# A two-layer decoder on one core: routing from the unnormalised sum, ranks built in another order, the last two experts normalised one by one

## The reference

```python
x = _layernorm(x + _L1_xattn_ref(x, ctx_1024, ...))        # CROSS1
probs = softmax(xf @ Wr)                                    # xf: 1024 x 128, Wr: 128 x 8
eidx = argmax(probs); p_tok = probs[eidx]
onehot = one_hot(eidx, 8)
rank = (cumsum(onehot, axis=0) - onehot)[eidx]              # tokens before this one in its expert
keep = rank < cap                                           # cap = 128
xe = xf[dispatch]                                           # 8 experts x 128 slots
ye = relu(xe @ W1) @ W2 * (p_tok[dispatch] * valid)
x = _layernorm(x + scatter_add(ye))
```

## Time and profile before

| What | Value |
|---|---|
| Median of the runs | 432.25 us (431.9 to 434.29) |
| Profiled execution, its time | 433.34 us |
| Profiled execution, span in the trace | 431.5 us |
| Mean granted clock of TensorE | 0.946 of full |
| Busy: PE, PEld, DVE, ACT, POOL | 372.1, 326.3, 282.8, 226.2, 53.8 us |

### The profile page before, as it was taken

The page is one execution under the profiler, slowest core; times in us unless marked ns, Lnnn a source line. Parts: engine busy times, 40 slices in busy tenths (PEclk is TensorE's granted clock), DMA queues, the critical chain, the costliest instruction groups (busy, mean ns, idle before and its releaser), DMA issues.

```text
span 431.5 us, 8936 instructions
## 1 busy us (share of the span) xinstructions
PE 372.1 (86%) x3188; PEld 326.3 (76%) x3188; DVE 282.8 (66%) x833; ACT 226.2 (52%) x526; POOL 53.8 (12%) x61
## 2 busy tenths in 40 slices
PE   4689898998999998999888999899999889863492
PEld 3577777886779997898876999788997677742391
DVE  6598889888955557532784455844866887825353
ACT  2145666764756565675347546584557455721241
POOL 6700005900000000000000000000002002010125
PEclk9989999999999999999969999999999979985597
DMA  5655320213330000200020000200021114700301
GB/s 162 187 182 161 111 58 17 75 54 111 122 111 2 2 2 1 74 2 2 4 71 2 2 0 2 74 2 2 1 56 32 51 24 152 230 35 0 109 13 33
DMA packets 22602, 25.14 MB, mean 58 GB/s; under 512 B 3224, under 2 KB 17313, under 8 KB 22560
## 3 DMA queue, kind: packets, MB, share of 16 engines
q1 hardware_dynamic: 21088, 22.95, 18.0%
q0 software_dynamic: 512, 0.97, 0.7%
q10 hardware_dynamic: 960, 0.66, 0.5%
HBM read 17.82 MB, written 6.83 MB: 57 GB/s over the span
## 4 chain that ended last, share of the span: by engine, by line
PE 71%; DVE 14%; issue 7%; DMA 3%; ACT 2%; POOL 1%; POOLq 0%; SPq 0%; ACTq 0%; DVEq 0%
PE bank_D L825 13%; PE bank_C L715 10%; PE bank_D L689 9%; PE bank_A L700 8%; DVE negmax L1208 4%; PE bank_A L841 4%; PE bank_A L843 3%; PE bank_A L842 3%; PE bank_D L615 2%; PE bank_D L673 2%; PE bank_A L755 2%; PE bank_D L745 1%; PE bank_A L635 1%; PE bank_A L1521 1%; PE bank_D L728 1%
## 5 line engine op out<-in xcount | busy, mean ns | idle before, releaser
L1208 DVE TENSOR_REDUCE negmax<-bank_D 128x2 f32<-128x512 f32 x192 | 127.6, 685 | 42.2 <-PE bank_D L689 42.0
L968 ACT ACTIVATE expo<-bank_A 128x512 f32<-128x512 f32 x192 | 110.3, 597 | 50.1 <-PE bank_A L700 48.0
L689 PE MATMUL bank_D<-k_head,q_sp 128*128 128x256 f32 x384 | 91.5, 324 | 10.0 <-DVE negmax L1208 5.3
L700 PE MATMUL bank_A<-q_sp,k_head 128*128 128x256 f32 x384 | 83.1, 302 | 4.9 <-DVE q_sp L1203 3.4
L1004 ACT ACTIVATE hidden<-bank_A,b 128x256 f32<-128x256 f32 x128 | 53.7, 471 | 52.1 <-PE bank_A L843 52.0
L689 PEld LDWEIGHTS bank_D<-k_head,q_sp 128*128 128x128 f32 x384 | 61.8, 200 | 22.3 <-issue 10.1
L825 PE MATMUL bank_D<-mix_w,hidden 128*128 128x128 f32 x512 | 67.8, 275 | 0.0
L700 PEld LDWEIGHTS bank_A<-q_sp,k_head 128*128 128x128 f32 x384 | 61.3, 196 | 7.7 <-DVE q_sp L1203 5.1
L825 PEld LDWEIGHTS bank_D<-mix_w,hidden 128*128 128x128 f32 x512 | 62.5, 191 | 1.6 <-issue 1.6
L715 PE MATMUL bank_C<-expo,v_aug 128*32 128x256 f32 x768 | 47.6, 389 | 2.0 <-ACT expo L968 1.6
L1267 DVE SCALAR_TENSOR_TENSOR y_mixture<-bank_D,g_w,y_mixture 128x128 f32<-128x128 f32 x64 | 22.3, 349 | 30.5 <-PE bank_D L825 28.8
(11 more groups left out here) (173 smaller groups left out, 511.1 us busy)
## 6 DMA issues: line engine op xcount, KB each, us to landing
mix_w<-in_mix_w SPq DMA_DIRECT2D x24, 256.0 KB, 3.6
k_head<-k_scratch SPq DMA_DIRECT2D x92, 48.0 KB
k_scratch<-qk_hi SPq DMA_DIRECT2D x24, 128.0 KB, 2.4
w_last<-in_mix_w SPq DMA_DIRECT2D x8, 256.0 KB, 6.4
k_scratch<-qk_lo SPq DMA_DIRECT2D x12, 128.0 KB, 2.3
proj_w<-in_proj SPq DMA_DIRECT2D x1, 640.0 KB, 5.2
xe_scratch<-empty_row SPq DMA_DIRECT2D x1, 520.0 KB, 4.7
expo<-xe_scratch SPq DMA_DIRECT2D x2, 260.0 KB, 3.2
```

Source lines behind the costliest of these rows:

```text
L689: last = mm(where(seq, b, ("max", k))[:, qt * SEQ:(qt + 1) * SEQ], q_sps[SET[seq, b]][:, k // 4, qt * P:(qt + 1) * P], k_heads[SET[seq, b] ...
L700: last = mm(where(seq, b, ("exp", h))[:, kt * SEQ:(kt + 1) * SEQ], k_heads[SET[seq, b]][:, t, g, kt * P:(kt + 1) * P], q_sps[SET[seq, b]][ ...
L968: activate(expo[:, exp_slot(seq, b, h), :], where(seq, b, ("exp", h))[:], ACT.Exp, scale=float(HD) ** -0.5).then_inc(free(seq, b, ("exp", ...
L1208: V.tensor_reduce(negmaxes[SET[seq, b]][:, s // 4, :, 32 * (s % 4)], where(seq, b, ("max", s))[:].rearrange("p (q n) -> p q n", q=QT), AX. ...
```

## The change

There are three parts. First, CROSS1 no longer transposes the normalised rows for the router but the sum before it (`transpose_sum`, step 32 instead of 34), with a router matrix whose column means are taken off. The logits are then those of the normalised rows except for the factor 1/std of the row, which doesn't alter the order; the exponential gets it later by a multiplication. Root and normalisation of CROSS1 move from steps 31 and 32 to 33 and 35, and ROUTE starts at step 34 instead of 35. Second, the counts matmuls come ahead of the wait for the onehot flags, one matmul with the triangle covers both tiles, another adds the first tile's flags to the second; the counts start at the expert's number instead of zero on each of 128 rows, so that the slot comes out of the sum directly, and are updated after the slot. The ranks move from step 2 to 3 of ROUTE, the exponential from 1 to 2; both stay at the same tick. Third, the groups of the last normalisation are 2, 2, 2, 1 and 1 experts.

```diff
 VALUES_AT = 17
-BACK_AT, CTX_AT, OUT_AT, ROOT_AT, NORM_AT, TURN_AT = 26, 28, 30, 31, 32, 34
-ATTENTION_STEPS = range(KEYS_AT, TURN_AT + 1)
+BACK_AT, CTX_AT, OUT_AT = 26, 28, 30
+ROOT_AT, NORM_AT, TURN_AT = 31, 32, 34
+SUM_TURN_AT, LAST_ROOT_AT, ROUTE_AT, LAST_NORM_AT = 32, 33, 34, 35
+ATTENTION_STEPS = range(KEYS_AT, LAST_NORM_AT + 1)
 GATE_AT, GATE_EXP_AT, GATE_WEIGHTS_AT, GATE_TURN_AT, BIAS_AT = 0, 1, 2, 4, 6
+CENTRE_AT = 3
...
     starts += [(at + len(MIXTURE_STEPS), CAUSAL1, seq) for seq, b, at in MIXTURE]
-    starts += [(at + TURN_AT + 1, ROUTE, seq) for seq, b, at in ATTENTION if b == CROSS1]
+    starts += [(at + ROUTE_AT, ROUTE, seq) for seq, b, at in ATTENTION if b == CROSS1]
...
                 turn(seq, b, "out", "D")
-            if s == TURN_AT:
+            if s == TURN_AT and b < CROSS1:
                 turn(seq, b, "xT", "A")
+            if s == SUM_TURN_AT and b == CROSS1:
+                turn(seq, b, "yT", "A")
...
                 turn(seq, b, "gate", "D")
+            if s == CENTRE_AT and (seq, b) == MIXTURE[0][:2]:
+                turn(seq, b, "centre", "D")
...
                 turn(seq, b, "logits", "D")
-            if s == 2:
+            if s == 3:
...
     c[:, C_ORDER:C_ORDER + QT * EXPERTS] = np.tile(EXPERTS - np.arange(EXPERTS), QT)
-    c[:, C_BASE:C_BASE + QT * EXPERTS] = np.tile(CAP * np.arange(EXPERTS), QT)
+    c[:, C_LIMIT:C_LIMIT + QT * EXPERTS] = np.tile(CAP * (1 + np.arange(EXPERTS)), QT)
+    c[:, C_FIRST:C_FIRST + EXPERTS] = np.arange(EXPERTS)
...
+                def transpose_sum(seq, b):
+
+                    wait_drained(pe, seq, b, "out")
+                    wait_free(pe, seq, b, "yT")
+                    for qt in range(QT):
+                        last = nc.tensor.transpose(where(seq, b, "yT")[:, qt * P:(qt + 1) * P],
+                                                   y[b][:, qt, :], ident)
+                    last.then_inc(full(seq, b, "yT"), 1)
...
                             output(seq, b, aT, wo[b])
-                        if s == TURN_AT:
+                        if s == TURN_AT and b < CROSS1:
                             transpose_x(seq, b)
+                        if s == SUM_TURN_AT and b == CROSS1:
+                            transpose_sum(seq, b)
...
                             last.then_inc(full(seq, b, "gate"), 1)
+                        if s == CENTRE_AT and (seq, b) == MIXTURE[0][:2]:
+                            pe.wait_ge(ld_const, 16)
+                            wait_free(pe, seq, b, "centre")
+                            mm(where(seq, b, "centre")[:, 0:EXPERTS], const[:, C_ONES:C_ONES + P],
+                               gate_w[:, 1, :], start=True, stop=True
+                               ).then_inc(full(seq, b, "centre"), 1)
...
                         if s == 0:
-                            wait_drained(pe, seq, CROSS1, "xT")
+                            wait_drained(pe, seq, CROSS1, "yT")
+                            wait_drained(pe, *MIXTURE[0][:2], "centre")
                             wait_free(pe, seq, b, "logits")
...
                                 last = mm(where(seq, b, "logits")[:, qt * EXPERTS:(qt + 1) * EXPERTS],
-                                          xT[seq][:, qt * P:(qt + 1) * P], gate_w[:, 1, :],
+                                          aT[:, qt * P:(qt + 1) * P], gate_c[:],
                                           start=True, stop=True)
                             last.then_inc(full(seq, b, "logits"), 1)
-                        if s == 2:
+                        if s == 3:
+                            wait_free(pe, seq, b, "rank")
+                            dst = where(seq, b, "rank")[:, 0:QT * EXPERTS]
+                            tri, ones = const[:, C_TRI:C_TRI + P], const[:, C_ONES:C_ONES + P]
+                            chosen = onehot[:, QT * seq:QT * (seq + 1), :].rearrange("p a e -> p (a e)")
+                            pe.wait_ge(counts_ready, seq + 1)
+                            for qt in range(QT):
+                                mm(dst[:, qt * EXPERTS:(qt + 1) * EXPERTS], ones, before[:, seq, :],
+                                   start=(qt == 0), stop=False)
                             pe.wait_ge(onehot_ready, seq + 1)
-                            wait_free(pe, seq, b, "rank")
-                            for qt in range(QT):
-                                dst = where(seq, b, "rank")[:, qt * EXPERTS:(qt + 1) * EXPERTS]
-                                mm(dst, const[:, C_TRI:C_TRI + P], onehot[:, QT * seq + qt, :],
-                                   start=True, stop=False)
-                                last = mm(dst, const[:, C_ONES:C_ONES + P], before[:, QT * seq + qt, :],
-                                          start=False, stop=True)
-                            last.then_inc(full(seq, b, "rank"), 1)
+                            mm(dst, tri, chosen, start=False, stop=False)
+                            mm(dst[:, EXPERTS:QT * EXPERTS], ones, onehot[:, QT * seq, :],
+                               start=False, stop=True).then_inc(full(seq, b, "rank"), 1)
...
                             copy_out(seq, b, "ctx", aT[:])
-                        if s == ROOT_AT:
+                        if s == (LAST_ROOT_AT if b == CROSS1 else ROOT_AT):
                             root(seq, b)
-                        if s == TURN_AT:
+                        if s == TURN_AT and b < CROSS1:
                             copy_out(seq, b, "xT", xT[seq])
+                        if s == SUM_TURN_AT and b == CROSS1:
+                            copy_out(seq, b, "yT", aT[:])
...
                     for s in ROUTE_STEPS:
-                        if s == 1:
+                        if s == 2:
...
                             moments(seq, b)
-                        if s == NORM_AT:
+                        if s == (LAST_NORM_AT if b == CROSS1 else NORM_AT):
...
                             weigh(seq)
+                        if s == CENTRE_AT and (seq, b) == MIXTURE[0][:2]:
+                            wait_filled(dve, seq, b, "centre")
+                            V.scalar_tensor_tensor(gate_c[:], where(seq, b, "centre")[:, 0:EXPERTS],
+                                                   -1.0 / P, gate_w[:, 1, :], ALU.mult, ALU.add
+                                                   ).then_inc(free(seq, b, "centre"), 1)
+                            V.tensor_copy(before[:, 0, :], const[:, C_FIRST:C_FIRST + EXPERTS]
+                                          ).then_inc(counts_ready, 1)
...
                     logits, diff, score, exps, work = (route[seq][:, i] for i in range(5))
-                    (greatest, first, total, weight, rank, base, beyond, number) = (
-                        route_col[seq][:, i, :] for i in range(8))
+                    (greatest, first, total, limit, number, beyond) = (
+                        route_col[seq][:, i, :] for i in range(6))
...
                     link(V.tensor_reduce(greatest, logits, AX.X, ALU.max))
-                    V.tensor_tensor(diff, logits, wide(greatest), ALU.subtract).then_inc(shifted, 1)
                     link(V.tensor_tensor(work, logits, wide(greatest), ALU.is_ge))
...
                     link(V.tensor_reduce(first, score, AX.X, ALU.max))
-                    link(V.tensor_tensor(onehot[:, tiles, :], score, wide(first), ALU.is_equal))
-                    for i in range(QT * seq, QT * (seq + 1)):
-                        last = V.tensor_tensor(before[:, i + 1, :], before[:, i, :], onehot[:, i, :],
-                                               ALU.add)
-                        if i == QT * seq:
-                            link(last)
-                    last.then_inc(onehot_ready, 1)
+                    V.tensor_tensor(onehot[:, tiles, :], score, wide(first), ALU.is_equal
+                                    ).then_inc(onehot_ready, 1)
+                    link(V.tensor_tensor(diff, logits, wide(greatest), ALU.subtract))
                     dve.wait_ge(onehot_ready, seq + 1)
                     link(V.tensor_tensor(work, onehot[:, tiles, :],
-                                         flags(const[:, C_BASE:C_BASE + QT * EXPERTS]), ALU.mult))
-                    V.tensor_reduce(base, work, AX.X, ALU.add)
-                    yield
-
-                    dve.wait_ge(routeexp_ready, seq + 1)
-                    link(V.tensor_reduce(total, exps, AX.X, ALU.add))
-                    V.reciprocal(x_rows[:, tiles, P + 1], total)
+                                         flags(const[:, C_LIMIT:C_LIMIT + QT * EXPERTS]), ALU.mult))
+                    V.tensor_reduce(limit, work, AX.X, ALU.add)
                     V.tensor_copy(x_rows[:, tiles, P],
                                   const[:, C_TOKEN + QT * seq:C_TOKEN + QT * (seq + 1)])
+                    yield
+
+                    V.tensor_tensor(diff, diff, wide(newton[CROSS1][:, 2, :]), ALU.mult
+                                    ).then_inc(shifted, 1)
+                    yield
+
```

(38 more changed lines are left out.)

## The result

The changed kernel takes 435.32 us in the median of 13 executions (432.77 to 436.66) against 432.25 for the kernel before, measured again beside it (13 executions, 431.11 to 434.8). The ratio is 1.0053, with a 95% interval of 1.0034 to 1.0071 (the quotient of the two medians is 1.0071; the times are two groups, and the median lies in the upper one). A second set gave 435.91 against 432.19, ratio 1.0073 [1.0051, 1.0096]. So it is slower, by 2.3 to 3.7 us, which is under 1%.

What follows compares the result with a forecast made beforehand. It took TensorE as the main bound (71% of the span, VectorE 14%), with the last sequence's routing alone on the path. Terms summed to +2.25 us on 433.34, giving 435.6, or 434.5 on the median; range 429.2 to 437.5.

Steps and rivals of the forecast that it cites:

- Last sequence: Sequence 3's routing: transpose waits for the sum alone (gain 2.65), logits to slot shortens (gain 0.45); together -3.1 us.
- End: Last normalisation and stores: expert 7's sum queues behind expert 6's whole chain on DVE, last store later, +0.55 us.
- Sequence 0: Moved router operations and normalisation delay the keys' low half on DVE; PE waits 2.2 us before score product 12; +2.0.
- The ranks' saving of 0.2: Sequence 0: the ranks then need no wait on PE, saving 0.2 us before 323.01.
- Sequence 1: DVE frees the values' projection's bank late, PE waits over 2 us, query shift comes later: +1.9 us.
- Sequence 2: Before the last value product: PE's wait for the counts goes, ACT's router exponential waits for the normalisation; -0.4 us.
- Clock: Sequences 0 and 1 together: new PE waits bring TensorE's lower clock level in dense work, +1.2 us (0 to 4).
- the prediction's reading of the formula: End: 58 cycles plus elements at 0.96 GHz, a Newton step estimated at 0.06 us; the end would gain 0.5 us.
- Rival (a): Stalls of sequences 0 and 1 hidden, last sequence's routing gain stays: -2.85, so 429.4 us; chance 0.22 together with (d).

Runs made afterwards that it cites:

- the run with the fill: Changed kernel plus overwritten TensorE products, 15 in sequence 0's wait and 22 in sequence 1's, against the kernel before: 433.26 us, ratio 1.0015.

## Why the prediction was right

Its sum was +2.25 us on the profiled execution, 434.5 for the median; the two medians measured are 435.3 and 435.9. The two waits and the last sequence's gain came as it said. That the sum came so near is in part luck, as the terms for sequence 1 and the clock show. Term by term:

- *Last sequence, -3.1*: from the sum to the slot 9.71 us became 6.52, **-3.19**. The transpose starts 0.48 after the sum, the score product at 2.94 after the logits' copy (2.96 said), the slot 3.82 after it (3.9 said). That the ranks' products ahead of the flags give nothing was 0.3 off, as the run with all of them behind shows.
- *End, +0.55*: **+0.58**. Expert 7's sum stands at 424.51 behind all of expert 6's chain.
- *Sequence 0, +2.0*: PE waits 2.05 (2.2 said) at the product named, and from the keys' projection to the shift it is 8.8 instead of 6.8: **+2.0**. The ranks' saving of 0.2 is in it.
- *Sequence 1, +1.9*: the wait was named with its place (2.91), but the stretch grew by **+1.4**. The logits ran at the full clock (0.51 us for four products, where 1.0 was taken), as did the products ahead of them, and the value projection started 9.8 us after the sequence's sum where the prediction has 11.7. So 1.9 was won, where the high clock at the logits had been priced at 0.8 (+1.1 in place of +1.9). The low clock from the end of the wait on then took 1.4 back: from the value projection to the query shift it is 5.6 us, where 4.15 was said, and the run with the fill gives back just this. Two errors of opposite sign leave the term only 0.5 off. With the clock full (23.4 us in the run with the fill) this piece is no longer than in the kernel before, which has a low stretch of 6.8 us in it.
- *Sequence 2, -0.4*: **-0.2**. ACT stood 1.63 us behind the router's exponential ("some 2").
- *Clock, +1.2*: this is the term that was mis-sized, and its place was half wrong. Beyond what sequence 1's term already holds, it is nothing in the lower group (some four of ten executions), and in the trace of one of the others +3.2 in sequence 1 and -1.4 behind value product 24. The sequence 0 wait, which the prediction counted as one "of that kind", is followed by the full clock in every trace taken, and filling it changed no piece of the trace.
- *Nothing was entered* for the work behind the slot. In the lower group's traces it gives back 0.8 of the last sequence's gain, at the lower clock.

Without the clock the sum was +1.05; the lower groups of the two sets (medians 432.9 and 433.2) stand 0.6 and 1.0 above the kernel before, and the upper ones (435.7 and 436.0) 2.8 above those. The forecast lay between the two, 1.3 to 1.6 above the one and 1.2 to 1.5 below the other, because a term of two values was entered as its middle. Which of the two the median shows was not foreseen.

The traces have six waits of 2.9 us in sequence 1, and the clock fell within each of them; in the run with both fills 1.4 us of this came back. They have six unfilled waits of 2.05 us in sequence 0, and the clock stayed full behind all of these. The Trainium skill (TensorE: Matmul & The Clock Gate, HAM oscillation) says that the cost of the transition is paid at every wait, but it says so of a kernel whose waits for transfers are about 3 to 5 us, longer than either wait here. So the prediction carried it too far when it said that by it both waits would cost; the case of 2.05 us goes against that reading.

In the changed end a Newton step takes 0.16 to 0.22 us, and the end lost 0.58 us, where the prediction's reading of the formula would have had it gain 0.5. The Trainium skill (VectorE: DVE Perf Modes, on the errata for sources in SBUF) gives that formula, but says right below it that it comes out too low and that the measured fixed term is about 150 cycles. With two elements that is an estimated 0.16 us, which agrees with the traces.

Rival (a), all stalls hidden, was priced at 429.4, close to what the kernel shows whose first three sequences keep the old order: 428.99. So what lies between (a) and the forecast is the queue on DVE, and the clock that goes with it.

## What to carry to other kernels

When a block of work is moved to another tick, list for the engine that runs it what stands behind it in program order, and for each of these the bank or buffer that it frees: 2.85 us of small DVE operations ahead of one 0.41 us operation made PE wait 2.05 and 2.91 us, and calling part of it two or three operations later took 2.85 us off these waits. Make the move only where the chain ends without cover (here the last sequence), and look for the idle time of the moved block's own engine to split it over. A cost that comes from the clock can have two values, as here: price both, and say which the median will see.

## What the runs showed of the hardware

- Kernels with the same opening have their first value product start between 31.4 and 33.7 us. Without a low stretch of the clock at 14 to 27 us it is 31.4 to 32.0, with one at 14 to 21 it is 32.1, with one at 23 to 27 it is 32.6 to 33.4, with both 33.7. One profile against another can't tell differences of this size unless such pieces are taken out.
- A stretch at the lower clock in sequence 1 lasts 3.4 us in one execution of the changed kernel and 17 us in another. In the long one PE is busy through its last 7.2 us, but for only 1.95 of the 4.00 us ahead of that. What ends such a stretch was not tested.
- In sequence 0 the full clock stayed behind an idle of 2.05 us on PE in all six traces that have it. In sequence 1 the clock fell within an idle of 2.9 us in all six traces that have it, and there was no low stretch in the two traces where it was filled. But in the same piece the clock also fell in the kernel before and in three others without any idle over 1.5 us ahead of the fall, so the length of an idle alone does not decide.
- Small operations that hang on each other, on 128x16 or 128x2 values, come at a pitch of 0.19 to 0.21 us on VectorE (0.25 behind the first Newton step), the same at both sizes.
